# Two of eight chunks projected ahead of the attention, six within it

## The reference

```python
x = x + _layernorm(_L0_attn_ref(_layernorm(x), W_dq, W_uq, W_dkv, W_uk, W_uv, W_o))
x = x + _layernorm(_L0_ffn_ref(_layernorm(x), wqkv, q_scale, k_scale, wo, ln_g, ln_b, w1, b1, w2, b2))

# _L0_attn_ref: 16 heads of 8, latent of 32
c_q = x @ W_dq;  Q = c_q @ W_uq
c_kv = x @ W_dkv;  K = c_kv @ W_uk;  V = c_kv @ W_uv
out = softmax(causal(Q @ K.T / sqrt(8))) @ V
return out @ W_o
```

## Time and profile before

| what | value |
|---|---|
| median of 3 runs (range) | 1354.26 us (1353.68 to 1358.48) |
| profiled execution, its span | 1356.70 us, 1355.0 us |
| mean granted clock of PE, as a share of full speed | 0.969 |
| PE busy in the span | 1233.4 us (91%) |
| DVE busy | 1121.9 us (83%) |
| ScalarE (ACT) busy | 925.5 us (68%) |
| GpSimd (POOL) busy | 745.5 us (55%) |

### The profile page before, as it was taken

One profiled execution on the slowest core, in us unless ns is written; L12 is line 12 of the kernel. 1 busy time (PEld: TensorE's weight loads), 2 busy tenths in 40 slices (PEclk: granted clock), 3 DMA queues, 4 the chain that ended last, 5 costly groups with the idle time before them and its releaser, 6 DMA issues. The chain is left out here.

```text
span 1355.0 us, 30203 instructions
## 1 busy us (share of the span) xinstructions
PE 1233.4 (91%) x10501; PEld 708.1 (52%) x10501; DVE 1121.9 (83%) x2928; ACT 925.5 (68%) x2463; POOL 745.5 (55%) x753
## 2 busy tenths in 40 slices
PE   4679999999999999888899999799899999997895
PEld 2423444434444443356566666565466666665663
DVE  5788998998899898679899999766589999997675
ACT  4515776877787677678888888533588888885344
POOL 1111211332231133478999999532699999997244
PEclk9859999999999999999999999899999999998998
DMA  4432111112111101011111111100112111111001
GB/s 105 125 112 75 45 51 51 59 55 57 46 39 54 48 16 35 25 39 41 32 33 33 33 27 31 48 0 1 24 25 54 33 33 33 26 32 25 1 17 47
DMA packets 35486, 56.46 MB, mean 42 GB/s; under 512 B 6898, under 2 KB 22652, under 8 KB 33020
## 3 DMA queue, kind: packets, MB, share of 16 engines
q1 hardware_dynamic: 34760, 54.39, 15.3%
q10 hardware_dynamic: 576, 0.15, 0.0%
HBM read 27.78 MB, written 8.39 MB: 27 GB/s over the span
## 5 line engine op out<-in xcount | busy, mean ns | idle before, releaser
L1128 ACT ACTIVATE a_prob<-a_psE 128x512 f32<-128x512 f32 (+1 forms) x608 | 303.8, 582 | 133.8 <-PE a_psE L740 131.0
L724 PE MATMUL a_psM<-a_ks,a_qs 72*128 72x512 bf16 (+3 forms) x768 | 241.9, 343 | 8.6 <-PEq L106 3.2
L740 PE MATMUL a_psE<-a_qs,a_ks 84*128 84x512 bf16 (+3 forms) x768 | 238.0, 334 | 12.7 <-ACT a_prob L1128 6.2
L1419 POOL TENSOR_TENSOR w_rn<-w_ssm,mhalf 128x16 f32<-128x16 f32 x64 | 220.4, 3444 | 48.7 <-DVE w_ssm L1619 33.4
L1360 POOL TENSOR_SCALAR_AFFINE_SELECT a_prob<-a_prob 128x512 f32<-128x512 f32 x128 | 81.1, 640 | 300.1 <-ACT a_prob L1128 293.1
L1527 DVE CUSTOM_DVE_ANT_0 a_psM<-a_psM,mask_q 128x384 f32<-128x384 f32 (+3 forms) x512 | 234.3, 523 | 13.2 <-PE a_psM L724 9.0
L1238 ACT ACTIVATE w_prob<-w_psS,w_bias 128x128 f32<-128x128 f32 x512 | 180.3, 378 | 21.0 <-DVE w_bias L1645 21.0
L1529 DVE TENSOR_REDUCE a_nm<-a_psM 128x1 f32<-128x512 f32 x256 | 158.9, 683 | 34.8 <-PE a_psM L724 33.8
L1404 POOL TENSOR_TENSOR w_t<-w_raw,w_sin 128x256 f32<-128x256 f32 x252 | 176.6, 732 | 0.0
L1409 POOL TENSOR_TENSOR w_rot<-w_t,w_t 128x1024 f32<-128x1024 f32 x63 | 148.7, 2360 | 8.6 <-issue 0.4
L740 PEld LDWEIGHTS a_psE<-a_qs,a_ks 84*128 84x128 bf16 x768 | 74.8, 98 | 145.0 <-ACT a_prob L1128 59.0
(11 more groups left out here) (189 smaller groups left out, 2391.5 us busy)
## 6 DMA issues: line engine op xcount, KB each, us to landing
a_qs<-q_parts SPq DMA_DIRECT2D x16, 576.0 KB
a_ks<-k_parts SPq DMA_DIRECT2D x16, 576.0 KB
q_parts<-p_parts SPq DMA_DIRECT2D x24, 128.0 KB
k_parts<-p_parts SPq DMA_DIRECT2D x24, 128.0 KB
w_vb__707<-w_v__691 SPq DMA_DIRECT2D x16, 128.0 KB, 2.2
w_vb__708<-w_v__691 SPq DMA_DIRECT2D x16, 128.0 KB, 2.3
w_vb__708<-w_v__692 SPq DMA_DIRECT2D x16, 128.0 KB, 2.2
w_vb__709<-w_v__692 SPq DMA_DIRECT2D x16, 128.0 KB, 2.4
```

Source lines behind the costliest of these rows:

```text
L724: mm = pe.matmul(psM[:, m_bank(r), at:at + n], qs[0:ROWS, g, j, i * P:(i + 1) * P], ks[0:ROWS, g, j, 512 * kc:512 * kc + n], start=True, s ...
L740: mm = pe.matmul(psE[:, r % NRING, j % share * w:(j % share + 1) * w], ks[0:KROWS, g, j, kt * P:(kt + 1) * P], qs[0:KROWS, g, j, q0:q0 + w ...
L1128: act.activation(prob[G % NPROB][:, j - share + 1:j + 1, 0:w], psE[:, r % NRING, 0:share * w].rearrange("p (j n) -> p j n", j=share), ACT. ...
L1419: pool.tensor_tensor(rn[:, T % 2, 0:n], ssm[:, T % 2, 0:n], sb["mhalf"][:, 0:n], ALU.pow).then_inc(rn_done, 1)
```

## The change

`project` takes only two chunks (`NFIRST`), and the parts have two places (`PARTS = 2`). Chunks 2 to 7 are projected in the attention, at six group numbers G; their steps are spread over the engines' lists from G - 5 to G + 6: DVE's `moments_c` at G - 5, GpSimd's `powers_x` at G - 4, DVE's `shift_c` at G - 3, ScalarE's `normal_x` at G - 2, PE's `turn_xn` and its copy at G, `project_heads` and two copies at G + 2, `project_tokens` and four copies at G + 3. All three cuts are GpSimd's now, out of SBUF: `cut_high` and `cut_low` of the queries at G + 3 and G + 4, of the keys at G + 5 and G + 6. Their psE slots come from the same ring of three. SP sends chunks 2 to 7 within stages 0 to 7, and the loads for stages 4 and later wait for both places. The pieces of wqkv are loaded in stages 10 to 13 instead of 4 to 7. At the end of the attention, `turn_x(3)`, `copy_hT(3)`, `rotate(1)`, `carry(3)`, `normalise(0)` and `sums(2)` change their places.

```diff
-PARTS = 4
+PARTS = 2
+NFIRST = 2
...
-            for c in range(PARTS):
+            for c in range(NFIRST):
                 sp.wait_ge(parts_done, 2 * c + 2)
                 send_parts(sp, io, sb, c)
...
-            sp.wait_ge(v_copied, 2)
             load_group(sp, io, sb, 0, 0)
-            for c in range(PARTS, 5):
-                sp.wait_ge(parts_done, 2 * c + 2)
-                send_parts(sp, io, sb, c)
...
+def chunk_group(c):
+
+    return (6, 14, 36, 46, 78, 86)[c - NFIRST]
...
+        for c in range(NFIRST, NCH):
+            for lag, names in ((0, "x"), (2, "qk"), (3, "v")):
+                if chunk_group(c) + lag == G:
+                    for name in names:
+                        slots[name, c] = n
+                        n += 1
...
+            def load_stage(s):
+                b = s // NG
+                for place in range(PARTS):
+                    sp.wait_ge(sb["parts_out"][place], 16 * 6 * (b + 1))
+                sp.wait_ge(av_done, (s - NG + 1) * NGR)
+                load_group(sp, io, sb, b, s % NG)
+
             load_group(sp, io, sb, 0, 1)
-            send_parts(sp, io, sb, 5)
             send_maxima(0, 0)
-            for c in range(6, NCH):
-                send_parts(sp, io, sb, c)
             send_maxima(0, 1)
...
+                if e > 1 and e + NG - 1 < NSTAGE:
+                    load_stage(e + NG - 1)
+                if e in (1, 4, 7):
+                    send_chunk((3, 5, 6)[(1, 4, 7).index(e)])
                 if e + 1 < NSTAGE:
                     send_maxima(e + 1, 1)
+                if e in (0, 3, 7):
+                    send_chunk((2, 4, 7)[(0, 3, 7).index(e)])
                 if e == 1:
+                    load_stage(NG)
                     load_weights(sp, io, sb)
-                if 4 <= e < 4 + W_PIECES:
-                    load_qkv_piece(sp, io, sb, e - 4)
+                if 10 <= e < 10 + W_PIECES:
+                    load_qkv_piece(sp, io, sb, e - 10)
...
+            def turn_xn(c):
...
+                for t in range(4):
+                    mm = pe.transpose(psE[:, r % NRING, t * P:(t + 1) * P], px_xn[:, t, :], sb["ident"])
...
+            def project_heads(c):
...
+                    pe.matmul(psE[:, r % NRING, :], sb["w_heads"][:, w, :], px_xnT[:, :], start=True, stop=True).then_inc(e_ready, 1)
+
+            def project_tokens(c):
...
+                for t in range(4):
+                    mm = pe.matmul(psE[:, r % NRING, t * P:(t + 1) * P], px_xnT[:, t * P:(t + 1) * P], sb["w_heads"][:, 2, :], start=True, stop=True)
...
-                if G == LAST_G - 2:
-                    pe.wait_ge(m_read, M_TAIL + 2)
-                    turn_x(3)
...
             project_qk(2)
+            pe.wait_ge(m_read, M_TAIL + 2)
+            turn_x(3)
...
+            def normal_x(c):
+
+                act.wait_ge(px_shift_done, c - NFIRST + 1)
+                if c > NFIRST:
+                    act.wait_ge(e_ready, E_SLOT["x", c - 1] + 1)
+                for t in range(4):
+                    i = act.activation(px_xn[:, t, :], sb["x"][:, c * 4 + t, :], ACT.Identity, scale=px_rstd[:, t:t + 1], bias=px_shift[:, t:t + 1])
...
+            def copy_heads(c):
+                ge(act, px_parts_done, 2 * (c - NFIRST))
+                for w in range(2):
...
+                    act.activation(px_full[:, w, :], psE[:, r % NRING, :], ACT.Copy).then_inc(e_read, 1)
...
+            def cut_high(c, w):
+
+                n, place = 2 * (c - NFIRST) + w, c % PARTS
+                pool.wait_ge(e_read, E_SLOT["qk"[w], c] + 1)
+                pool.wait_ge(sb["parts_out"][place], 16 * 6 * (c // PARTS))
+                pool.tensor_copy(sb["parts"][:, place, w, 0, :], px_full[:, w, :]).then_inc(px_high_done, 1)
+                pool.wait_ge(px_high_done, n + 1)
+                ge(pool, px_parts_done, n)
+                pool.tensor_tensor(px_rem[:, :], px_full[:, w, :], sb["parts"][:, place, w, 0, :], ALU.subtract).then_inc(px_rem_done, 1)
+
+            def cut_low(c, w):
+
+                n, place = 2 * (c - NFIRST) + w, c % PARTS
+                pool.wait_ge(px_rem_done, n + 1)
+                pool.tensor_copy(sb["parts"][:, place, w, 1, :], px_rem[:, :]).then_inc(px_mid_done, 1)
+                pool.wait_ge(px_mid_done, n + 1)
+                pool.tensor_tensor(sb["parts"][:, place, w, 2, :], px_rem[:, :], sb["parts"][:, place, w, 1, :], ALU.subtract).then_inc(px_parts_done, 1)
...
-                if runs(s + 1):
+                if runs(s + 1) and T != 1:
                     sums(T + 1)
...
+                if G == LAST_G - 3:
                     rotate(1)
                     carry(3)
-                if G == LAST_G - 2:
-                    copy_hT(3)
-                if G == LAST_G - 1:
                     normalise(0)
...
+            copy_hT(3)
             outputs(NSTAGE - 1, 1)
+            sums(2)
             dve.memset(kT[:, :, :, 0:WIN], 0.0).then_inc(zeroed, 1)
```

## The result

The changed kernel takes 1369.59 us (median of 4 runs, 1367.96 to 1371.60) against 1354.94 for the kernel before (4 runs, 1353.68 to 1358.48): a ratio of 1.0106 with a 95% interval of 1.0089 to 1.0124. It is slower by 14 to 15 us, 1.1%; 1355.8 was forecast, in a range from 1345 to 1367, and the median lies above that range.

The account below looks back on a forecast made before the run. PE was taken to bound a plain stage, a queue the start. The terms -20.9 - 1.4 + 19.1 + 6.1 + 1.0 - 2.4 sum to +1.5, giving 1355.8 us against the median of 1354.26, range 1345 to 1367.

Parts of the forecast that it names:

- The start: Up to the first score: projecting only two chunks ahead lets the first load go earlier, -20.9 us, bounds -18 and -25.
- the 49 give or take 2: At the start: a sign of the forecast, the time in us at which the first maxima would run.
- Stage 1's wait of 1.38: At stage 1's first score: the wait for maxima behind two loads would go, -1.4 us.
- Six chunks on PE: In the attention's stages: PE's turns, heads and token products take 3.2 us a chunk, paid in full, +19.1 us.
- Rings, DVE and ACT: In the attention's stages: added DVE and ACT steps and score ring slots, 1.0 us a chunk, +6.1 us, between 0 and +12.
- POOL's cuts: On GpSimd in the attention: cuts fit idle time, but late powers delay shifts and maxima, +1.0 us, between 0 and +4.
- the two upper bounds together: In the attention's stages: +12 us if extra ACT work costs twice as much, and +4 us for late powers.
- The sign that was named for it: In the attention: stages growing by less than 3 or more than 5.5 us would make the prediction wrong.
- The tail: At the end of the attention: PE's wait at tile 3 goes, -3.7, sums(2) adds +1.3, together -2.4 us.
- ACT's queue blocked: Rival, in the attention: chunk copies in ACT's order hold up exponentials and so PE, 1364.7 us, chance 0.15.
- The cuts slowing DVE: Rival, in the attention: POOL's cuts running beside DVE's maxima stretch them, +9 us, 1364.8 us, chance 0.10.
- SP's order: On SP in the attention: sends of six chunks between maxima and loads cost 0, some 1.4 us if one came late.

Follow-up runs that it names:

- pfns: Changed kernel with GpSimd's powers ahead of the cuts, chunks 6 and 7 at groups 84 and 94, and ScalarE's normals in two pairs: span 1354.1 us.
- pf: Changed kernel with GpSimd's powers of a chunk ahead of the mask and cuts instead of behind them: span 1363.3 us.
- ms: Changed kernel with a chunk's moments on DVE in two pieces, two tiles a group earlier and two in their old group: span 1371.3 us.
- sbk: Changed kernel with DVE's sums(2) back in its old place: to the sixth norms 37.56 us, from the last copy of outputs to the end 778.66.
- lw: Changed kernel in which SP issues the second load only when the first has landed: span 1364.7 us.
- again: Changed kernel profiled once more, with no edit: span 1367.7 us.
- tail_only: Kernel before the change with only the edits at the end of the attention: span 1354.5 us.
- g84: Changed kernel with chunks 6 and 7 moved from groups 78 and 86 to 84 and 94, their sends a stage later: span 1360.4 us.
- cd: Changed kernel with all cuts of chunks 2 to 7 on DVE instead of GpSimd, at the same groups: span 1378.1 us.

## Why the prediction was wrong

*The start* was nearly right: -18.84 for -20.9, inside its bounds of -18 and -25. The load was issued 1.7 later than I took and took 0.4 longer, and the maxima's DMA is waited for 3.26 instead of 4.15 (0.9 less, as taken). The first maxima at 51.26 are just outside the 49 give or take 2 that was named as a sign. Stage 1's wait of 1.38 is gone, as said.

*Six chunks on PE* were right: 3.0 for a chunk on PE where 3.2 was said, paid in full in the stage (chunks 4 and 5, and all six in pfns).

*Rings, DVE and ACT* is the step that failed, together with *POOL's cuts*, its +1.0 for late powers. I priced a chunk's moments and normals by batch 0's norms, as busy time that adds up, 0.8 a step (six times that and the 0.2 are 6.0, not 6.1). What they cost depends on where they stand: 1.2 us of moments, a shift that waits 2.2 for GpSimd, or 1.6 us of normals, each in one piece ahead of maxima or exponentials, stop PE, as the rings behind which PE works are three (scores) and four (maxima) slots deep. For the normals `pf` and `pfns` show it, for the moments `ms` in part. The wait for the powers was named and its length nearly right (two of 1.9 forecast, 2.23 each, and a third of 2.44 for chunk 2), but taking it away shortens PE's stop by only 0.12. What was missing is what follows: PE's stops of 1.3 to 1.5, and behind most of them stretches at half clock of 3.4 to 10.2 us, which cost more than the stop (1.6 to 4.5 by the stretches above). The two terms measure 34.2 - 19.1 + 1.4 = 16.5, where I took 7.1. Of the 9.4 between them, 5.4 are the half clock in stages 6 and 7 (by `sbk` and `lw`) and 1.4 that in chunk 2's row (by `again`), and the stops themselves lie behind the rest, in part at least. Even the two upper bounds together, +12 and +4, fall just short of it, as one was ACT's work counted twice, the other two waits, and neither had a loss of clock in it. The sign that was named for it came true: a stage that grows by more than 5.5, stage 6 by 10.9. (The bounds of the sum reach to 1371.9 if all are taken, not to 1370.)

*The mistake in reading*: I had the clock in the earlier trace rows (the values of 2.59 after a stop of 2.05, at a granted clock of 0.50 from 570.7 to 574.1) and used it for the tail alone. The same row was the warning for every stop that the change adds.

*The tail* was right: -3.52 + 1.45 = -2.1 for -2.4, and tail_only shows it on the kernel before.

*The rivals.* ACT's queue blocked, 1364.7 at 0.15, was nearest in its mechanism, though it named the copies of the heads and not the normals: pf shows the stop by normals, and pfns shortens it to 0.59; but DVE's queue had as large a part. The cuts slowing DVE, at 1364.8 as near in its number, was wrong. The cuts don't slow DVE's maxima: the masked and the plain maxima take 521 and 681 ns in the changed kernel, beside 42 us of cuts, and 523 and 683 before:

```profile
L1654 DVE CUSTOM_DVE_ANT_0 a_psM<-a_psM,mask_q 128x384 f32<-128x384 f32 (+3 forms) x512 | 234.1, 521 | 44.1 <-PE a_psM L747 39.8 <-POOL a_nmp L1473 3.9
L1656 DVE TENSOR_REDUCE a_nm<-a_psM 128x1 f32<-128x512 f32 x256 | 158.8, 681 | 40.8 <-PE a_psM L747 39.8 <-issue 0.2
```

The contention that the Trainium skill ("GPSIMD Engine Reference", 1. Specifications) names for two inputs in SBUF is not seen on these operations, which read PSUM and at most one tile of SBUF. SP's order cost nothing, as said: behind the first outputs PE waits for no DMA in the changed kernel's attention.

What stays open: why the clock falls behind some stops and not behind others that are as long; and what the moments' stop in stage 6 (1.27) and the normals' (1.26) cost each, since g84 moved both away from batch 0's norms.

## What to carry to other kernels

Work that is moved into a stage is priced in two parts: its time on the engine that bounds the stage, which is paid anyway, and the longest piece in which it stands in another engine's list ahead of what that engine feeds; where that piece is longer than the ring between them, it is a stop, and a stop can cost one to three times its own length more in clock (3.8 behind one of 1.46). Ahead of a move, look at what the resource that is freed would wait for next: here PE had 29 us of idle time at the start, so the chunks that were moved away from it could have stayed, once their sends no longer stood ahead of the load.

## What the runs showed of the hardware that was not expected

Stops of PE of 0.9 to 1.9 us within a stage that is else busy are followed by a stretch at half clock (granted 0.50), or not, from one execution to the next:

- In stage 1, the stop of 1.48 us was followed by none in the changed kernel's first profile. In the seven other runs with a stop of over 1 us there, 6.8 us followed in `again` (1.47), `pf` (1.36), `sbk` (1.47) and `cd` (1.13), and 10.2 us in `g84` (1.47), `lw` (1.48) and `ms` (1.87).
- In stage 7, 10.2 us followed in the changed kernel (1.47), `again` (1.46), `ms` (1.86) and `cd` (1.12), 6.8 in `lw` (1.47), and none in `pf` (1.35) and `sbk` (1.46).
- In stage 6, the stop of 1.27 behind the moments was followed by 3.4 us in five runs and by none in `lw`; one of 0.89 (`ms`) by 3.4. The second stop of that stage, 1.16 to 1.28 behind normals, was followed by none in all seven runs that have it.
- A stop of 0.59 (`pfns`, stage 1), and those of 0.92 to 0.93 in stage 3, were followed by none.

So one profile does not tell what a stop costs: the changed kernel's first profile lacks the fall in stage 1 that all seven others have.
